# Weights loaded in layer 0's tail, gates in buffers of their own, five banks for the tail's products, normalising bank by bank

## What is computed

```python
# layer 0, recurrent: gates of all steps at once, then a scan over 256 steps
gates = einsum('bsd,gd->bsg', x, W) + b; f, i, o, z = split(gates)
c = sigmoid(f) * c + sigmoid(i) * tanh(z)
h = sigmoid(o) * tanh(layer_norm(c))
# layer 0, feed-forward: a tree of depth 5, fan 4, 4 trees; a token walks it by argmax
act = gelu(x @ W_in.T + b_in); out = (act * mask_of_visited_nodes) @ W_out.T
# layer 1, delta rule, 16 heads of 8, scan over 256 steps
q, k, v = silu(conv4(hidden @ W{q,k,v}.T)); q, k = l2norm(q) * d**-0.5, l2norm(k)
S = S * exp(g_t); S = S + outer(k_t, (v_t - k_t @ S) * beta_t); o_t = q_t @ S
out = (rmsnorm(o) * silu(hidden @ Wg.T)) @ Wo.T
# layer 1, two transformer layers: local attention, window 64, 8 heads of 64
q, k = rotary_xpos(l2norm(q) * q_scale, l2norm(k) * k_scale)
attn = softmax(where(mask, -max, q @ k.T * 8)); x = x + (attn @ v) @ wo
a, g = split(layer_norm(shift(x)) @ w1 + b1); x = x + (a * gelu(g)) @ w2 + b2
```

## Time and profile before

| | us |
|---|---|
| median of 3 runs | 1553.08 (1552.3 to 1557.53) |
| profiled execution | 1555.76 |
| its span, first to last instruction | 1554.0 |
| layer 0 | 0 to 626 |
| preparing | 628 to 750 |
| local phase | 752 to 1554 |

### The profile page before, as it was taken

How to read it: one execution, slowest core, us unless ns; L and a number is a source line. 1 busy time by engine, 2 the same in 40 slices (tenths; PEclk the granted TensorE clock), 3 DMA queues, 4 the chain that set the end, 5 groups by cost and what they waited for, 6 DMA issues and landing times.

```text
span 1554.0 us, 31376 instructions
## 1 busy us (share of the span) xinstructions
PE 1306.3 (84%) x9368; PEld 886.8 (57%) x9368; DVE 1296.0 (83%) x4362; ACT 1235.3 (79%) x3431; POOL 938.0 (60%) x1472
## 2 busy tenths in 40 slices
PE   5888878888797666897489999999999999999986
PEld 3555646566565443343256666666666666666665
DVE  3278897979888895488299999999999999999985
ACT  2367877979787886587289989989989989999985
POOL 0237464464645651078488778778778778777752
PEclk9999999999988856898699999999999999999998
DMA  3359677686868773499301101111101111111233
GB/s 111 107 183 335 222 280 248 218 297 213 314 204 285 286 274 109 136 286 315 122 22 34 44 11 44 43 44 34 43 13 44 44 44 34 19 36 44 67 94 111
DMA packets 156505, 210.33 MB, mean 135 GB/s; under 512 B 68272, under 2 KB 109616, under 8 KB 156208
## 3 DMA queue, kind: packets, MB, share of 16 engines
q0 software_dynamic: 36864, 134.76, 24.9%
q1 hardware_dynamic: 119040, 71.98, 16.8%
q10 hardware_dynamic: 432, 1.59, 0.3%
HBM read 168.97 MB, written 26.74 MB: 126 GB/s over the span
## 4 chain that ended last, share of the span: by engine, by line
PE 26%; ACT 14%; issue 6%; DVE 4%; POOL 2%; ACTq 0%; DVEq 0%; POOLq 0%
ACT lo_s_ps L1743 6%; PE lo_h_ps L1558 4%; PE lo_qk_ps L1454 4%; PE lo_s_ps L1510 3%; PE lo_o_ps L1548 2%; DVE prepared_then_rounds L2082 2%; ACT L1830 2%; ACT prepared_then_rounds L1801 2%; PE lo_ft_ps L1530 2%; PE lo_v_ps L1460 2%; PE lo_h_ps L1568 1%; PE lo_s_ps L1497 1%; PE lo_h_ps L1530 1%; ACT prepared_then_rounds L1751 1%; PE lo_o_ps L1530 1%
## 5 line engine op out<-in xcount | busy, mean ns | idle before, releaser
L334 POOL DMA_INDIRECT l_rows<-in_table,l_idx x256 | 256.5, 1002 | 293.9 <-DVE l_idx L795 131.4
L639 ACT ACTIVATE l_rows<-l_rows,l_act 128x128 f32<-128x128 f32 x1024 | 306.6, 390 | 2.1
L753 DVE CUSTOM_DVE_ANT_0 l_rows<-l_rows,xn_tok 128x128 f32<-128x128 f32 x1024 | 299.7, 362 | 6.5 <-DMA l_rows<-in_table,l_idx 4.9
L1743 ACT ACTIVATE lo_s_ps<-lo_s_ps,lo_nmx,lo_rn 128x128 f32<-128x128 f32 x504 | 219.7, 440 | 1.3 <-DVE lo_nmx L2066 0.9
L473 PE MATMUL l_acc<-ident,l_rows 128*128 128x128 f32 x1024 | 163.0, 307 | 55.6 <-ACT l_rows L639 34.3
L473 PEld LDWEIGHTS l_acc<-ident,l_rows 128*128 128x128 f32 x1024 | 129.4, 157 | 92.0 <-ACT l_rows L639 54.6
L439 PE MATMUL l_S<-pre,l_AT 128*128 128x144 f32 (+3 forms) x832 | 130.3, 308 | 25.9 <-ACT l_AT L630 24.7
L439 PEld LDWEIGHTS l_S<-pre,l_AT 128*128 128x128 f32 (+2 forms) x832 | 117.5, 208 | 56.4 <-ACT l_AT L630 40.0
L1454 PE MATMUL lo_qk_ps<-wqkv,lo_hT 128*128 128x512 f32 x256 | 126.6, 618 | 22.8 <-DVE lo_c L2056 11.5
L415 PE MATMUL l_log<-l_xT,top_in 128*128 128x512 f32 (+1 forms) x192 | 118.6, 711 | 19.1 <-issue 9.2
L1933 POOL TENSOR_TENSOR lo_de_kS<-lo_de_S,lo_de_ops 128x384 f32<-128x384 f32 x128 | 128.0, 1000 | 10.0
(11 more groups left out here) (321 smaller groups left out, 3376.8 us busy)
## 6 DMA issues: line engine op xcount, KB each, us to landing
lo_VE<-lo_V SPq DMA_DIRECT2D x64, 128.0 KB, 2.8
scratch_ops<-prepared_then_rounds SPq DMA_DIRECT2D x4, 1792.0 KB, 7.5
lo_de_ops<-scratch_ops SPq DMA_DIRECT2D x16, 448.0 KB, 4.2
l_rows<-in_table,l_idx POOLq DMA_INDIRECT x256
scratch_qo<-prepared_then_rounds SPq DMA_DIRECT2D x8, 512.0 KB, 8.7
lo_de_qo<-scratch_qo SPq DMA_DIRECT2D x16, 256.0 KB, 4.6
x_tok<-in_x SPq DMA_DIRECT2D x8, 256.0 KB, 5.2
scratch_x<-x_tok SPq DMA_DIRECT2D x8, 256.0 KB
```

The lines of the kernel that those rows point to most:

```text
L334: pool.indirect_dma_start(rows[L][:, r % SLOTS, p, :], None, a[f"table{L}"], bass.IndirectOffsetOnAxis(ap=at[:, p:p + 1], axis=0)).then_in ...
L639: ins = act.activation(z, z, ACT.Copy, scale=actv[L][:, r % 2, k:k + 1])
L753: ins = dve.tensor_tensor_reduce(z, z, x, 1.0, bias, ALU.mult, ALU.add, accum_out=pick[L][:, r % 2, k:k + 1])
L1743: ins = act.activation(here, here, ACT.Exp, scale=rn[:, v % 2, j, 2 * k + e:2 * k + e + 1], bias=nmx[:, j, e, k:k + 1], accum_out=sums[:, ...
```

## The change

The change has six parts. L numbers are those of the kernel before.

- **A.** ACT loads its table of functions for gelu at its very start, ahead of its first wait, instead of loading one table at L646 and another at L630.
- **B.** z(0) to z(6) go to five banks (two `log_ps`, two halves of `S`, `gate_ps`) instead of two. z(0) to z(4) move one round ahead on PE and wait for two more semaphores, by which those banks are free. ACT copies z(0) and z(1) between `tanh_n` and `tanh_f`, and the other five behind `tanh_f`.
- **C.** A buffer `wide`, resident over all phases, holds first `rows[4]`, then layer 1's weights, the q and k of the local phase and its table `tab`. SP issues the eight loads of weights in layer 0, when tile 31 of the first table has been spread. Only qk_scale, rot and mask are still loaded in preparing.
- **D.** The weighting by taps moves from the start of preparing to DVE's work in the last round but one of layer 0 (`weigh_taps`, ahead of the last `raise_f`), in place. PE no longer waits for `made`.
- **E.** The gates get eight buffers of their own in qT and kT, which are not used until the local phase; `silu_gate` waits for no store, and the wait at SP's end goes. The same wait now stands in the local phase, ahead of ACT's first copy of q (`keep_q(0, 0)`) and ahead of SP's loads of the gates at the end.
- **F.** Normalising goes bank by bank: for each (unit, j) two reciprocals of 128x4 and two products of 128x512, where there were one of 128x8 and one of 128x1024; the semaphore counts four a unit, and PE's turning and ACT's exponentials wait for their own bank.

```diff
+        z_ps = [log_ps[0][:], log_ps[1][:], S[:, 0:2, :]..., S[:, 2:4, :]..., gate_ps[:]]
...
-            for h in range(3, NG):
+            for h in range(3, NG - 1):
                 keep_x(h)
+            sp.wait_ge(spread[4].sem, spread[4].after(NT - 1))
+            for k in WEIGHTS:
+                sp.dma_start(m[k], a[k]).then_inc(weights_in, 16)
+            keep_x(NG - 1)
...
+            sp.wait_ge(weights_in, 16 * len(WEIGHTS))
...
                 if h == 0:
                     pe.wait_ge(pre_early, 16 * len(PRE_EARLY))
+                    pe.wait_ge(log_kept.sem, len(order))
+                    pe.wait_ge(ftop_kept.sem, ftop_kept.after(NG - 1))
+                    pe.wait_ge(gate_kept.sem, gate_kept.after(NG - 1))
                 pe.wait_ge(m_kept.sem, m_kept.after(h))
-                if h >= 2:
-                    pe.wait_ge(z_kept.sem, z_kept.after(h - 2))
+                if h >= NZ:
+                    pe.wait_ge(z_kept.sem, z_kept.after(h - NZ))
...
             for g in range(NG + 5):
+                for h in range(NZ) if g == NG + 3 else ():
+                    z(h)
...
+            act.preload_act_table_set("gelu_and_others")
             act.wait_ge(halved.sem, 1)
...
+                for h in (0, 1) if g == NG + 2 else ():
+                    keep_z(h)
+                if on(g - 3):
                     tanh_f(g - 3)
-                for h in range(NG - 1) if g == NG + 2 else ():
+                for h in range(2, NG - 1) if g == NG + 2 else ():
                     keep_z(h)
...
+                if g == NG + 3:
+                    weigh_taps()
                 if on(g - 4):
                     raise_f(g - 4)
...
-            sp.wait_ge(gate_stored.sem, gate_stored.after(NG - 1))
-            pe.wait_ge(made.sem, 1)
-            pe.wait_ge(late.sem, 16 * len(m["late"]))
...
                 act.wait_ge(gated.sem, gated.after(g))
-                if g < 6:
-                    act.wait_ge(y_stored[x].sem, y_stored[x].after(n))
...
+                if (v, i) == (0, 0):
+                    act.wait_ge(m["gate_stored"].sem, m["gate_stored"].after(NG - 1))
...
+                for e in (0, 1):
+                    at, n = slice(e * NP, (e + 1) * NP), 2 * j + e + 1
+                    if v:
+                        dve.wait_ge(pn_ready.sem, pn_ready.after(v - 1, n))
+                    dve.wait_ge(prob_ready.sem, prob_ready.after(v, n))
+                    dve.reciprocal(rsum[:, j, at], sums[:, j, at]).then_inc(rsum_ready.sem, 1)
+                    dve.wait_ge(rsum_ready.sem, rsum_ready.after(v, n))
+                    if v:
+                        dve.wait_ge(pt_full.sem, pt_full.after(v - 1, n))
+                    dve.tensor_tensor(prob[:, j, e], z, rsum[:, j, at]..., ALU.mult).then_inc(pn_ready.sem, 1)
```

105 lines of the change are left out of this document (53 added, 52 removed).

## The result

| | before | after |
|---|---|---|
| median of 16 runs each, us | 1554.15 (1549.68 to 1562.36) | 1547.11 (1538.3 to 1559.37) |
| ratio after / before, 95% interval | | 0.9951 [0.9931, 0.9971] |
| profiled execution, us (its span) | 1555.8 (1554.0) | 1547.07 (1545.3) |

A forecast was written before the change was run, and what follows sets the result against it. No single engine bounds the whole; DVE nearly bounds the local phase. From the 1553.1 us median, -1.3 - 3.1 + 0.4 - 1.95 - 7.2 - 6 - 0.7 = -19.9 gives 1533.2; range 1526 to 1546.

The forecast's parts named there:

- F, loop and last unit: Local phase, normalising by bank: -6 us over 30 units of the loop (-11 to +1), and -0.7 in the last unit.
- the step that priced the even share: Layer 0's tail: weights and gathers share 410 GB/s evenly, tile 31's rows +1.2 us, slack takes 1.1; +0.4 taken.
- the far end of the forecast (+3.9): Layer 0's tail: if all weights went ahead of the gathers, these end at 600.5, costing +3.9 us after slack.
- the second rival: Layer 0's tail: weights push tile 31's gathers back by the full price, +3.9 instead of +0.4: 1536.7 us; chance 0.07.
- the first rival: Local phase: split normalising brings nothing, DVE becomes the bound; 0 to +8 us there, 1540 to 1548 overall; chance 0.2.
- The price on DVE: Local phase: two reciprocals and two 512-wide products take 1.70 us instead of 1.40, +0.3 a pair, +0.6 a unit.
- it starts 0.37 earlier, 23.17: Local phase, PE's turn L1530: with the first bank ready sooner it starts 0.37 us earlier, making the unit 23.17 us.
- The third rival: Local phase: DVE saturated, no stalls go, split normalising costs +20 to +30 us, 1560 to 1570 overall; chance 0.06.
- -0.7: Local phase's last unit: two waits for ACT on the chain, 0.4 and 0.7 us, shrink by the split; -0.7 us taken.
- all such pairs at 0.06: Whole kernel: chance 0.06 that gains of two parts fail together and 1549 to 1557 us comes out.
- signs named for being wrong: Unit of 23.6 us or more; DVE waiting over 1 us for tile 31's rows; local phase starting under 10 us earlier.
- the 23.4 and the 23.6 that were to decide: Local phase: units of 23.2 to 23.4 us would show the forecast right, 23.6 or more wrong.

The follow-up runs named there:

- run 11: The pairs kernel with late weights (run 5) without the early table load: 0.9939 of before, median 1510.14 us.
- run 12: Same code as run 5, repeated as control (late weights, normalising in pairs): 0.9927 of before, median 1509.45 us.
- run 4: After, with the eight weight loads held until tile 31's last gather has landed: 0.9904 of before, median 1539.95 us.
- run 6: Run 4 with taps weighted at preparing's start and SP's gate-store wait at its end, as before: 0.9955 of before, median 1516.84 us.
- run 5: Run 4 with normalising in pairs exactly as before, semaphore steps of one: 0.9898 of before, median 1507.99 us.
- run 7: Run 4 with normalising split by bank only for j = 1, and j = 0 a pair: 0.9911 of before, median 1508.84 us.
- run 9: After, weights still early, with wqkv loaded by four transfers and w1 by two, in shorter pieces: 0.9947 of before, median 1510.52 us.
- Run 2: After, with ACT's copy of o ahead of the two squares in each unit: 0.9972 of before, median 1552.26 us.
- Run 10: Run 5 with three extra unused 512-wide PE products at preparing's end: 0.9923 of before, median 1508.5 us.

## Why the prediction was right or wrong

| part | forecast | found | by |
|---|---|---|---|
| A, table load | -1.3 | -1.4 to -1.7 at the first scaling; -0.8 and -2.2 at the last gather, within the wander | traces, runs 11 and 12 |
| B, z in five banks | -3.1 | -3.3, and 0.6 given back | traces |
| C, weights in the tail | +0.4 | +4.2 | run 4 |
| D and E, taps and gates | -9.15 | -9.2; 8.6 to 9.5 with late weights | run 6 |
| F, loop and last unit | -6.7 | 0 | runs 5 and 7 |
| start of the local phase | 0 | +2.0, in part PE's low clock | traces |

With the forecast's A, -1.3 - 3.3 + 0.6 + 4.2 - 9.2 + 1.2 (the whole local phase, F and its start together) = -7.8, beside the -7.6 measured. That they agree so closely is luck: with the -2.2 of the traces in A's place it is -8.7, and the interval goes from -4.5 to -10.7.

**B** went as worked out: ACT's scaling right behind DVE's, the first five products in PE's gap, ten matmuls 0.43 us apart, so 4.3 us, the end of the 4.2 to 8.3 that full clock gives, and the spread behind them not delayed (0.23 idle ahead of it, for ACT's scaling). What was not foreseen is that PE is now idle 3.66 us ahead of the last turn, where it was idle 2.22, and runs it at a granted clock of 0.50 (1.2 GHz; 619.8 to 621) instead of 0.96 (619.5 to 622 before), 1.12 us for what took 0.66: most of the +0.6.

**C** failed at the step that priced the even share: "Shared evenly, they take 2.0 x 2 / 0.41 = 9.8 us, to 596.8: +1.2", of which the slack was to take 1.1. Two things in it were wrong. The first is that I took even to be even in bytes. The Trainium skill, "DMA: Bandwidth & Descriptors", section "Queues, rings and completion order", says that the engines take turns between queues packet by packet. The trace agrees from 590 us on: 301 packets of weights to 305 of gathers up to 596; in the four us before it is 115 to 81. (Whether the profile counts the same packets as the Trainium skill isn't shown.) Nothing follows from this for equal bytes, and they were not equal, since a packet of weights held 2.4 times as much. At 1.83 MB in 6 us the 3.52 MB of weights take 11.5 us, from 583.2 to about 595, and in 6 us of that time the gathers get 0.64 MB; so most of the weights went ahead of the last gathered rows, close to the far end of the forecast (+3.9) and to the second rival. The second is that the even share itself was priced too low. In run 9, with short pieces, the gathers got 1.39 MB to the weights' 0.99, and the stage still took 3.1 us more than with late weights, where an even share was to cost 0.1 to 0.4. Hardly a gathered row moved there after 562.5 (9 packets), and DVE started at 564.80; how the 3.1 us divide among the bandwidth, the first two us, in which the weights led, and that last stretch stays open. That 594 to 596 was empty before did not help: after, 0.83 MB moved in that stretch, and DVE's wait ended at 598.56.

**D and E** were right to 0.05 us in the two traces, and their signs in the profile came as named: PE at the phase's start, no wait for the gate stores, ACT's first steps of the local phase waiting for PE.

**F** was the largest error, and it was the first rival: "the split brings nothing". The price on DVE was slightly high: a half is 0.81 from start to start (1022.15 to 1022.96), so 1.62 a pair beside 1.39, +0.23 and not +0.3. The estimate by the Trainium skill, "Perfetto Trace Analysis", section "Optimizing Scalar/DVE Operations", was +0.19, which is nearer. The step that failed is "it starts 0.37 earlier, 23.17", by which a unit would shorten because one wait on it is gone; it stayed at 23.53. Measured from the start of the unit's norm on ACT, `lo_lnv` (997.37 before, L1768; 1012.70 after, L1782), with the first of the two reciprocals in after:

| after `lo_lnv`, us | before | after | earlier by |
|---|---|---|---|
| DVE's reciprocal, j = 1 | 9.94 | 9.45 | 0.49 |
| PE's turn of probabilities | 11.46 | 10.92 | 0.54 |
| PE's turn of q, second half | 11.95 | 11.91 | 0.04 |

The before column's rows, with PE's turn of the earlier trace rows, are these:

```profile
997.37 0.47 ACT L1768 ACTIVATE lo_lnv<-lo_h_ps,cols 128x256 f32<-128x256 f32 x1 [0.15 <-PE lo_h_ps L1568]
...
1008.51 0.64 ACT L1757 COPY prepared_then_rounds<-lo_o_ps 128x512 f32<-128x512 f32 x1
...
1009.32 0.60 PE L1482 MATMUL lo_o_ps<-ident,lo_c 128*128 128x128 f32 x4
```

PE's turn came half a us earlier, and the very next one stood still, because it needs ACT's copy of o, which ends at the same time as ever: 1008.51 + 0.64 before, only 0.17 ahead of PE's turn, hidden there behind the wait for DVE. I had looked at the wait ahead of PE's step and not at when the inputs of the step behind it are ready. Run 2 moves that copy, and PE's wait goes while DVE's grows. The third rival, which feared that DVE's longer work lengthens the unit, fell too: the extra work went where DVE had waited for the exponentials. That the split is worth nothing is shown (runs 5 and 7 against run 4). That PE, ACT and DVE close the loop among them within 0.2 us, so that removing one wait moves it to the next, fits runs 2, 5 and 7 but is argued; which chain sets 23.53 is not shown.

In the last unit -0.7 did not come either: from the 30th root to the end it is 61.36 in both.

**The start of the local phase** had no term at all. The first group of rows is from after, the second from before:

```profile
751.33 3.78 PE L1468 MATMUL lo_qk_ps<-wide,lo_hT 128*128 128x512 f32 x4 [3.72 <-DVE lo_c L2072]
...
784.10 3.25 PE L1468 MATMUL lo_qk_ps<-wide,lo_hT 128*128 128x512 f32 x4 [2.29 <-DVE lo_c L2072]
```

```profile
761.28 3.33 PE L1454 MATMUL lo_qk_ps<-wqkv,lo_hT 128*128 128x512 f32 x4 [3.31 <-DVE lo_c L2056]
...
792.15 1.95 PE L1454 MATMUL lo_qk_ps<-wqkv,lo_hT 128*128 128x512 f32 x4 [1.70 <-DVE lo_c L2056]
```

The second group of products starts 9.3 us into the phase in both. The granted clock is 0.50 there after (751 to 757) and 0.66 before (761 to 766), and q's first turn comes 14.57 us into the phase after and 13.67 before: 0.9 of the 2.0. The fifth group takes 3.25 us at a granted clock of 0.61 (784.1 to 788.5) after and 1.95 at 1.00 (792.15 to 795) before; the fourth went the other way, 1.98 after and 2.90 before. Run 10, the only other one with its first root as late (59.39), has the same 14.57, with 3.31 for the fifth group; runs 6, 7 and 12, at 57.6 to 57.8, have 13.7 and 1.96. So the stretches in which PE runs at half clock are a good part of this spread. How the rest divides, and why the clock falls at other places from run to run, no run shows.

**The range.** Its high end took the rivals in one at a time. The first and the second came true together, 0.2 and 0.07, and I had put all such pairs at 0.06; with the start of the local phase on top the time passed 1546 by 1. That small distance says little: before itself was measured at 1554.15 here, 1.05 above the median that the sum started from. Of the signs named for being wrong two appeared: DVE's wait for tile 31's rows, and a local phase that starts 9.94 us earlier where less than 10 was the mark. The unit of 23.53 lies between the 23.4 and the 23.6 that were to decide.

**What stays open**: whether A lasts to the end of layer 0, what in the even share cost 3 us in run 9, which chain sets the unit's 23.53, and what besides the clock makes the local phase's first unit take 57.6 to 59.4 us after and 57.35 before.

**The version to keep** is after with run 4's wait, split or not: 0.9904 (split), 0.9911 (split in one half), 0.9898 and 0.9927 (pairs), some 14 us below before. That is 6 us more than the change's own gain, and the trace of C accounts for 4.2 of it; the intervals leave 3 us either way.

## What to carry to other kernels

A wait that stands on the path is worth no more than the distance to the next input of the step behind it: before pricing its removal, look up when the inputs of the next two instructions on that engine are ready, not only when the engine is free. A prefetch beside transfers that somebody waits for should be priced by packets, with the longer ones taking the larger share of the bytes; here it cost 3 us even with short ones. It should be held back by one wait until the last urgent transfer has landed if its own cover allows it. When rivals are independent, price them together as well, since the range is missed when two small ones come true at once.
